# Conv weights built on GpSimd, only the borders of the conv input cleared, loads begun at once, last stores shared by two queues

## The chip, the cores and the metric

The kernel runs on 1 core of one Trainium2 chip. The metric is the time of one execution on the device, in microseconds (us). The engines are TensorE (PE in the profile), VectorE (DVE), ScalarE (ACT), GpSimd (POOL) and SyncE (SP); SP and ACT also issue DMAs, each on a queue of its own.

## The reference

One pre-activation layer, `x + attention(groupnorm(x))`, over x of shape (8, 512, 128, 128), f32. The 512 channels are 32 groups of 16, so there are 256 (image, group) pairs, all independent:

```
x = x + conv_ref(_gn(x), ...)
# conv_ref, for each group gx of 16 channels:
gap, gmp = mean(gx), max(gx) over (h, w)
channel_weight = sigmoid(gn(conv1x1([gap, gmp], w_cc, b_cc)))
hw = conv1x1([mean over w, mean over h], w_s1, b_s1)
pos_h, pos_w = sigmoid(conv1x1(hw[:h], w_ph, b_ph)), sigmoid(conv1x1(hw[h:], w_pw, b_pw))
sx = conv3x3(gx * pos_h * pos_w, w_s3, b_s3)      # 16 -> 16 channels, zero padding
spatial_weight = sigmoid(gn(sx))                  # per channel over (h, w)
out = gx * (channel_weight * spatial_weight)
```

## The kernel before, in words

**Layout.** A group (16 channels of 128x128) fills the 128 partitions: 16 channels times 8 row phases, with 16 rows of 128 pixels in each partition. A unit is two groups, j = 0 and 1, in 2 MB of `xt`; there are 128 units, and `xt` holds six of them. One group comes in by 8 DMAs of 128 KB, one for each row phase, and goes out by 8.

**Turns.** `turns` writes the program out for t = -5 to 128. In turn t the engines work on different units: t + 3 (unit e, row sums and maxima on DVE), t + 2 (c, position sums), t + 1 (a, gates, gate products on POOL, `modulate` on DVE), t (the 3x3 convolution on PE, its eviction on ACT) and t - 1 (b, spatial gate and final sums). DVE has its first unit in turn -3, PE its first convolution in turn 0; turn 128 (`t == UNITS`) only finishes unit 127. Every engine runs its list in order and waits on semaphores; nothing is scheduled at run time.

**Queues.** SP loads the weights (three DMAs), then group j = 1 of each unit, and stores everything. Its loads of units 0 to 5 wait for nothing, so 48 DMAs are issued in a row. ACT loads group j = 0 of each unit, spread over its compute; first it waits for the three weight DMAs (`w_in`) and seven memsets of POOL (`w_pool`), then issues units 0 and 1 (16 DMAs) and comes to `square1` of unit 0, which needs `negm` from DVE. Loads of unit 6 and later wait for `final` of the unit six earlier.

**Setup.** DVE expands every weight table from `weights` and `masks` with small instructions: `expand` makes a 128x128 table by four instructions of 128x32. The convolution's `W_conv` (three of 128x128) is nine expansions and six additions. The helper `link` makes DVE wait after each instruction for its own completion. PE then forms five products of tables (`w_pe`), DVE takes six results out of them, and clears the whole padded convolution input `gated` (9360 elements a partition), of which only the borders must be zero, since `gate_products` writes the inside of every unit. Only then does DVE turn to its first `row_sums`.

**End.** In turn 128 ACT runs, for unit 127: `variance2(b, 0)`, `square2(b, 1)`, `spatial_gate(b, 0)`, `variance2(b, 1)`, `spatial_gate(b, 1)`, `gate_plus_one(b, 1)`. `variance2` needs a product of PE and hands its value to POOL's `rstd2_power`, on which the `spatial_gate` of the same group waits. DVE follows with `gate_x` and `add_x` for j = 0, `gate_x` and `add_mean` for j = 1; each ends a group (`final`), and SP stores it.

## Time and profile before

| | |
|---|---|
| time, median of 3 runs | 3395.1 us (3390.4 to 3396.04) |
| time of the profiled execution | 3391.47 us |
| its span, first to last instruction | 3389.6 us |
| DVE busy | 97% of the span |
| PE busy | 95% |
| ACT busy | 90% |
| POOL busy | 75% |
| mean granted TensorE clock | 0.994 of full speed |

The span covers instructions alone; the time has 1.9 us more around it. Four numbers of this table (the three runs and the profiled one) lie within 5.7 us of each other for one and the same kernel.

### The profile page before, as it was taken

How to read it: one execution, taken by the hardware profiler on the slowest of the kernel's cores; microseconds unless marked ns; L12 is line 12 of the kernel's file. 1: busy time of each engine (PE TensorE's matmuls, PEld its weight loads, DVE VectorE, ACT ScalarE, POOL GpSimd, SP SyncE). 2: the span in 40 equal slices, each digit the busy share in tenths (PEclk: the TensorE clock that was granted, in tenths of full speed). 3: DMA queues.
4: the chain of work that ended last, by engine and by line, in shares of the span. 5: the costliest groups of instructions: out<-in, count | busy, mean ns of one | idle time of the engine just before them, and what ended most of it. 6: DMA issues, size and time to landing. Idle time of an engine off the chain costs nothing.

```text
span 3389.6 us, 125024 instructions
## 1 busy us (share of the span) xinstructions
PE 3212.1 (95%) x51732; PEld 1483.5 (44%) x51732; DVE 3288.2 (97%) x1997; ACT 3050.6 (90%) x5634; POOL 2542.6 (75%) x1548
## 2 busy tenths in 40 slices
PE   2999999999999999999999999999999999999996
PEld 1444444444444444444444444444444444444442
DVE  8999999999999999999999999999999999999984
ACT  1899999999999999999999999999999999999986
POOL 2777777887787777777787777777777777778872
PEclk9999999999999999999999999999999999999998
DMA  5467676776776767677677677667767767667755
GB/s 127 113 163 165 167 170 157 169 172 157 168 172 162 167 169 167 160 169 173 155 169 175 155 168 173 162 163 171 169 159 172 171 157 168 169 160 168 173 112 101
DMA packets 1115102, 545.32 MB, mean 161 GB/s; under 512 B 65712, under 2 KB 1114544, under 8 KB 1114544
## 3 DMA queue, kind: packets, MB, share of 16 engines
q1 hardware_dynamic: 836016, 403.05, 52.3%
q10 hardware_dynamic: 278528, 134.28, 14.9%
q8 instruction: 417, 6.83, 0.9%
q14 instruction: 141, 1.16, 0.1%
HBM read 268.63 MB, written 268.44 MB: 158 GB/s over the span
## 4 chain that ended last, share of the span: by engine, by line
DVE 58%; issue 23%; PE 7%; POOL 5%; ACT 3%; SPq 1%; DMA 1%; ACTq 1%; DVEq 0%; POOLq 0%
DVE mx L659 13%; DVE sp_buf L607 13%; DVE sums L644 12%; DVE gated L699 8%; DVE fold L632 6%; PE conv_ps L747 6%; DVE fold L636 2%; SPq L237 1%; DMA out<-sp_buf 1%; POOL rstd L327 1%; ACT sp_buf L393 1%; POOL rstd L266 1%; DVE sp_buf L617 1%; POOL var_e L308 1%; ACTq L382 1%
## 5 line engine op out<-in xcount | busy, mean ns | idle before, releaser
L747 PE MATMUL conv_ps<-gated,W_conv 64*32 64x512 f32 x49152 | 2803.4, 590 | 2.8 <-issue 1.6
L747 PEld LDWEIGHTS conv_ps<-gated,W_conv 64*32 64x32 f32 x49152 | 1126.3, 105 | 1492.5 <-issue 1461.2
L285 POOL TENSOR_TENSOR gated<-gate_w,gate_hr 128x2048 f32<-128x2048 f32 x256 | 1053.9, 4117 | 10.1
L393 ACT ACTIVATE sp_buf<-conv_ps,weights 128x512 f32<-128x512 f32 x1024 | 692.0, 678 | 148.3 <-DMA out<-sp_buf 120.6
L607 DVE SCALAR_TENSOR_TENSOR sp_buf<-xt,negm,sp_buf 128x2048 f32<-128x2048 f32 x256 | 600.3, 2345 | 42.6 <-ACT sp_buf L455 26.8
L699 DVE SCALAR_TENSOR_TENSOR gated<-xt,negm,gated 128x2048 f32<-128x2048 f32 x256 | 594.8, 2364 | 13.9 <-POOL gated L285 13.9
L327 POOL TENSOR_TENSOR rstd<-var_e,consts 128x4 f32<-128x4 f32 x129 | 389.0, 3015 | 273.4 <-DVE var_e L686 273.2
L644 DVE TENSOR_REDUCE sums<-xt 128x32 f32<-128x4096 f32 x128 | 564.9, 4413 | 0.1
L659 DVE TENSOR_REDUCE mx<-xt 128x2 f32<-128x4096 f32 x128 | 564.4, 4409 | 0.2 <-issue 0.2
L447 ACT ACTIVATE sp_buf<-sp_buf,bias,scale 128x2048 f32<-128x2048 f32 x256 | 536.9, 2097 | 8.5
L465 ACT ACTIVATE junk<-xt,negm 128x2048 bf16<-128x2048 f32 x256 | 512.5, 2002 | 28.3 <-DVE negm L693 28.3
L416 ACT ACTIVATE junk<-sp_buf,negm 128x2048 bf16<-128x2048 f32 x256 | 512.8, 2003 | 8.3
L266 POOL TENSOR_TENSOR rstd<-var_e,consts 128x1 f32<-128x1 f32 x256 | 305.4, 1193 | 246.5 <-ACT var_e L430 246.5
L617 DVE SCALAR_TENSOR_TENSOR sp_buf<-sp_buf,kfac,xt 128x2048 f32<-128x2048 f32 x128 | 301.1, 2352 | 4.5
L632 DVE TENSOR_TENSOR fold<-xt 128x2048 f32<-128x2048 f32 x128 | 292.1, 2282 | 0.0
L455 ACT ACTIVATE sp_buf<-sp_buf,consts,kfac 128x2048 f32<-128x2048 f32 x128 | 268.7, 2099 | 4.3
L308 POOL TENSOR_TENSOR var_e<-ch,consts 128x2 f32<-128x2 f32 x128 | 261.0, 2039 | 10.1 <-POOL ch L304 0.2
L274 POOL TENSOR_TENSOR gate_hr<-gate_h,rstd 128x32 f32<-128x32 f32 x128 | 114.1, 891 | 190.7 <-ACT gate_w L480 175.2
L393 ACT ACTIVATION_READ_ACCUMULATOR sp_buf<-conv_ps,weights 128x1 f32 x1024 | 201.4, 197 | 0.0
L295 POOL TENSOR_TENSOR fold<-fold 128x512 f32<-128x512 f32 x128 | 164.0, 1281 | 47.4 <-DVE fold L636 47.4
L747 PE MATMUL gn_ps<-late_in,M_chan 128*128 128x21 f32 x264 | 53.7, 281 | 129.4 <-ACT sp_buf L393 83.0
L626 DVE TENSOR_SCALAR sp_buf<-sp_buf,negm 128x2048 f32<-128x2048 f32 x128 | 164.7, 1287 | 4.5
(84 smaller groups left out, 2256.0 us busy)
## 6 DMA issues: line engine op xcount, KB each, us to landing
out<-sp_buf SPq DMA_DIRECT2D x2048, 128.0 KB, 2.8
xt<-in_x SPq DMA_DIRECT2D x1024, 128.0 KB, 3.7
xt<-in_x ACTq DMA_DIRECT2D x1024, 128.0 KB, 3.6
weights<-in_by_channel SPq DMA_DIRECT2D x1, 116.5 KB, 2.1
S_chan<-in_same_channel SPq DMA_DIRECT2D x1, 64.0 KB, 1.9
masks<-in_row_masks SPq DMA_DIRECT2D x1, 12.0 KB, 2.1
```

What stands on the lines that cost most here:

```text
L285: nc.gpsimd.tensor_tensor(gated[:, d, j, 1:1 + NB, 1:1 + W], gate_w[:, d, j].unsqueeze(1).to_broadcast([P, NB, W]), gate_hr[:, d, j].unsqu ...
L327: nc.gpsimd.tensor_tensor(rstd[:, s, first:4], var_e[:, s % 2, first:4], consts[:, first:4], ALU.pow).then_inc(rstd_done, 1)
L393: nc.scalar.activation(sp_buf[:, g, k * BB:(k + 1) * BB], conv_ps[:, k], ACT.Identity, bias=V["b_s3"], accum_out=sums2).then_inc(evac, 1)
L416: nc.scalar.activation(junk[:, 2], sp_buf[:, g].rearrange("p b w -> p (b w)"), ACT.Square, bias=negm2[:, g:g + 1], accum_out=squares).then ...
L447: nc.scalar.activation(flat, flat, ACT.Sigmoid, scale=scale2[:, g:g + 1], bias=bias2[:, g:g + 1]).then_inc(sig2, 1)
L465: nc.scalar.activation(junk[:, j], xt[:, s, j].rearrange("p b w -> p (b w)"), ACT.Square, bias=negm[:, s, j:j + 1], accum_out=all_in[:, (s ...
L607: nc.vector.scalar_tensor_tensor(flat, xt[:, s, j].rearrange("p b w -> p (b w)"), negm[:, s, j:j + 1], flat, ALU.add, ALU.mult).then_inc(f ...
L632: nc.vector.tensor_tensor(fold8[:], xt[:, s, :, 0:8], xt[:, s, :, 8:16], ALU.add).then_inc(fold8_done, 1)
L644: nc.vector.tensor_reduce(sums[:, s % 2].rearrange("p j b -> p (j b)"), xt[:, s].rearrange("p j b w -> p (j b) w"), AX_X, ALU.add).then_in ...
L659: nc.vector.tensor_reduce(mx[:, s % 2], xt[:, s].rearrange("p j b w -> p j (b w)"), AX_X, ALU.max).then_inc(mx_done, 1)
L699: nc.vector.scalar_tensor_tensor(inner, xt[:, s, j], negm[:, s, j:j + 1], inner, ALU.add, ALU.mult).then_inc(mod_done, 1)
L747: return nc.tensor.matmul(ps, lhsT, rhs, start=start, stop=stop)
```

## The change

Four things, all in the first turns or the last.

1. `W_conv` is expanded by POOL (36 small multiplications, then two additions over all 384 columns), after DVE has done its own tables. PE waits for it (`w_conv`) ahead of its first convolution.
2. POOL clears the borders of `gated` with four memsets; DVE's memset of all of it is gone. `link` no longer waits; DVE waits once inside its tables and once ahead of the six results, and these are taken in turn -3, behind the first `row_sums` and `totals`.
3. ACT's wait for `w_in` and `w_pool` moves from its beginning to turn -2, so its first 16 loads wait for nothing; a one-column Sigmoid (`warm`) follows that wait.
4. In turn 128 `variance2(b, 1)` comes ahead of `spatial_gate(b, 0)`, and the last unit's 16 stores are split: for each group SP issues four and ACT, after its last activation, four.

```diff
+            for s in range(2):
+                nc.gpsimd.memset(gated[:, s, :, 0:NB + 2:NB + 1, :], 0.0).then_inc(w_pool, 1)
+                nc.gpsimd.memset(gated[:, s, :, 1:1 + NB, 0:WP:WP - 1], 0.0).then_inc(w_pool, 1)
+            pool.wait_ge(w_pool, POOL_SETUP)
             pool.wait_ge(w_in, 16 * W_LOADS)
+            pool.wait_ge(w_dve, DVE_FIRST)
+            for kw in range(KW):
+                made = expand_conv(W_conv[:, kw], wconv_rep[:, kw, 1], masks[:, 1], made)
+                for i, kh in enumerate((0, 2)):
+                    made = expand_conv(w_part[:, i, kw], wconv_rep[:, kw, kh], masks[:, kh], made)
+            for i in range(2):
+                pool.wait_ge(w_conv, made)
+                nc.gpsimd.tensor_tensor(W_conv[:], W_conv[:], w_part[:, i], ALU.add).then_inc(w_conv, 1)
...
         def _(act):
-            act.wait_ge(w_in, 16 * W_LOADS)
-            act.wait_ge(w_pool, 7)
...
+                if t == -2:
+                    act.wait_ge(w_in, 16 * W_LOADS)
+                    act.wait_ge(w_pool, POOL_SETUP)
+                    nc.scalar.activation(warm[:, :], consts[:, 8:9], ACT.Sigmoid)
...
+                if t == UNITS:
+                    variance2(b, sb_, 1)
                 if real(b):
                     spatial_gate(b, sb_, 0)
...
-                if real(b):
+                if real(b) and t < UNITS:
                     variance2(b, sb_, 1)
...
             turns(act, body)
+            last_stores()
...
                 made[0] += 1
                 ins.then_inc(w_dve, 1)
-                dve.wait_ge(w_dve, made[0])
...
-            for kw in range(KW):
-                expand(W_conv[:, kw], wconv_rep[:, kw, 1], masks[:, 1])
-                for i, kh in enumerate((0, 2)):
-                    expand(w_part[:, i, kw], wconv_rep[:, kw, kh], masks[:, kh])
-                    link(nc.vector.tensor_tensor(W_conv[:, kw], W_conv[:, kw], w_part[:, i, kw], ALU.add))
...
-            link(nc.vector.memset(gated[:].rearrange("p s j b w -> p (s j b w)"), 0.0))
...
+                    if t == 0 and n == 0:
+                        pe.wait_ge(w_conv, CONV_SETUP)
```

DVE's program, from the last tables to the first `maxima`; before:

```order
L588 TENSOR_SCALAR mask_pix<-masks 128x8 [waits w_dve]
L590 COPY W_rows_m<-pos_ps 128x128 [waits w_pe,w_dve]
L591 COPY W_cols_m<-pos_ps 128x128 [waits w_dve]
L592 TENSOR_SCALAR W_rows<-pos_ps 128x128 [waits w_dve]
L593 TENSOR_SCALAR W_cols<-pos_ps 128x128 [waits w_dve]
L594 TENSOR_TENSOR W_gap_m<-W_gap_m,norm_ps 128x128 [waits w_dve]
L595 TENSOR_TENSOR b_pos<-pos_ps,weights 128x2 [waits w_dve]
L597 MEMSET gated 128x9360 [waits w_dve]
L644 TENSOR_REDUCE sums<-xt 128x32 [waits x_in01,x_in00,w_dve]
L653 TENSOR_REDUCE all_in<-sums 128x2 [waits sums_done]
L659 TENSOR_REDUCE mx<-xt 128x2
```

and of the change, the same place (its line numbers are 48 or 49 higher in the turns):

```order
L631 TENSOR_TENSOR W_ch_m<-W_gap,W_gmp 128x128 [waits w_dve]
L632 TENSOR_SCALAR W_gap_m<-W_gap 128x128
L693 TENSOR_REDUCE sums<-xt 128x32 [waits x_in01,x_in00,w_pool]
L702 TENSOR_REDUCE all_in<-sums 128x2 [waits sums_done]
L640 COPY W_rows_m<-pos_ps 128x128 [waits w_dve,w_pe]
L641 COPY W_cols_m<-pos_ps 128x128
L642 TENSOR_SCALAR W_rows<-pos_ps 128x128
L643 TENSOR_SCALAR W_cols<-pos_ps 128x128
L644 TENSOR_TENSOR W_gap_m<-W_gap_m,norm_ps 128x128
L645 TENSOR_TENSOR b_pos<-pos_ps,weights 128x2
L708 TENSOR_REDUCE mx<-xt 128x2
```

The memset is gone, the six results stand behind the first two reductions, and the first reduction waits for both groups of unit 0 (`x_in00`, `x_in01`).

ACT's program at the very end, unit 127; before:

```order
L416 ACTIVATE junk,late_in<-sp_buf,negm 128x2048 [waits sq2_done,evac,negm2_done]
L439 ACTIVATE scale<-rstd,weights 128x1 [waits sig2,rstd2_done]
L442 ACTIVATE bias<-negm,weights,scale 128x1 [waits aff2]
L447 ACTIVATE sp_buf<-sp_buf,bias,scale 128x2048 [waits sq2_done,aff2]
L430 ACTIVATE var_e<-gn_ps,consts 128x1 [waits rstd2_done,late_mm]
L439 ACTIVATE scale<-rstd,weights 128x1 [waits sig2,rstd2_done]
L442 ACTIVATE bias<-negm,weights,scale 128x1 [waits aff2]
L447 ACTIVATE sp_buf<-sp_buf,bias,scale 128x2048 [waits sq2_done,aff2]
L455 ACTIVATE sp_buf<-sp_buf,consts,kfac 128x2048 [waits kfac_done,sig2]
```

and of the change:

```order
L457 ACTIVATE junk,late_in<-sp_buf,negm 128x2048 [waits sq2_done,evac,negm2_done]
L471 ACTIVATE var_e<-gn_ps,consts 128x1 [waits rstd2_done,late_mm]
L480 ACTIVATE scale<-rstd,weights 128x1 [waits sig2,rstd2_done]
L483 ACTIVATE bias<-negm,weights,scale 128x1 [waits aff2]
L488 ACTIVATE sp_buf<-sp_buf,bias,scale 128x2048 [waits sq2_done,aff2]
L480 ACTIVATE scale<-rstd,weights 128x1 [waits sig2,rstd2_done]
L483 ACTIVATE bias<-negm,weights,scale 128x1 [waits aff2]
L488 ACTIVATE sp_buf<-sp_buf,bias,scale 128x2048 [waits sq2_done,aff2]
L496 ACTIVATE sp_buf<-sp_buf,consts,kfac 128x2048 [waits kfac_done,sig2]
L423 DMA out<-sp_buf 256x1x128 [waits final]
L423 DMA out<-sp_buf 256x1x128 x3
```

The variance of the last group (`var_e<-gn_ps`) has moved ahead of the other group's scale, bias and Sigmoid, and stores follow the last activation.

## Rows read from the trace of the kernel before

**Rows 1.** Windows, mid-run: busy PE, PEld, DVE, ACT, POOL; clock, DMA share, GB/s.

```profile
1000.00:1026.00 26.00, 25.27 (x420) 11.49 (x412) 25.82 (x16) 24.20 (x46) 19.75 (x13) 1.00 0.67 163
```

**Rows 2.** Timeline of DVE, setup: start us, busy us, line, operation, count, idle before.

```profile
3.81 0.87 DVE L565 TENSOR_TENSOR W_conv<-weights,masks 128x32 f32<-128x32 f32 x4 [3.81 <-DMA masks<-in_row_masks]
...
13.89 0.87 DVE L565 TENSOR_TENSOR W_s1h<-weights,masks 128x32 f32<-128x32 f32 x4
...
20.09 0.17 DVE L588 TENSOR_SCALAR mask_pix<-masks 128x8 f32<-128x8 f32 x1
22.73 0.29 DVE L590 COPY W_rows_m<-pos_ps 128x128 f32<-128x128 f32 x1 [2.46 <-PE pos_ps L740]
...
26.52 7.86 DVE L597 MEMSET gated<- 128x9360 f32 x1 [2.02 <-issue]
34.42 4.42 DVE L644 TENSOR_REDUCE sums<-xt 128x32 f32<-128x4096 f32 x1
```

**Rows 3.** SP's line of loads, its first eight: ns, issue times, us to landing.

```profile
L229 SPq DMA_DIRECT2D xt<-in_x x8: 592/608/736, 2.1 to 6.8; - x8
...
DMA to landing us min/median/max: 2.7/4.1/5.8
```

**Rows 4.** The same view of ACT's line of loads, its first eight.

```profile
L382 ACTq DMA_DIRECT2D xt<-in_x x8: 622/630/680, 3.8 to 8.5; - x8
...
DMA to landing us min/median/max: 3.6/5.4/6.8
```

**Rows 5.** Windows again: loads on two queues, and the last stores on one.

```profile
10.00:12.00 2.00, 0.00 (x0) 0.00 (x0) 1.73 (x9) 0.00 (x0) 0.00 (x0) 1.00 1.23 226
...
3386.00:3388.00 2.00, 0.00 (x0) 0.00 (x0) 0.00 (x0) 0.00 (x0) 0.00 (x0) 0.50 1.00 199
```

**Rows 6.** Timeline of the whole core, turn -2 to turn 0.

```profile
48.56 1.27 POOL L295 TENSOR_TENSOR fold<-fold 128x512 f32<-128x512 f32 x1 [47.36 <-DVE fold L636]
...
58.48 0.61 PE L747 MATMUL pos_ps<-sums,W_rows 128*128 128x32 f32 x2
...
62.05 1.28 ACT L475 ACT_TABLE_LOAD   x1 [13.01 <-POOL rstd L327]
...
64.74 0.24 POOL L274 TENSOR_TENSOR gate_hr<-gate_h,rstd 128x32 f32<-128x32 f32 x1 [2.78 <-ACT gate_w L480]
65.06 7.17 POOL L285 TENSOR_TENSOR gated<-gate_w,gate_hr 128x2048 f32<-128x2048 f32 x2
...
71.46 0.81 DVE L664 TENSOR_TENSOR late_in<-mx,mask_pix 128x16 f32<-128x16 f32 x1
...
77.23 8.86 PE L747 MATMUL conv_ps<-gated,W_conv 64*32 64x512 f32 x120
```

**Rows 7.** One POOL line over the whole run: ns min/median/max.

```profile
L274 POOL TENSOR_TENSOR gate_hr<-gate_h,rstd x128: 238/970/1257, 64.7 to 3314.5; 128x32 f32<-128x32 f32 x128
```

**Rows 8.** Timeline of DVE: one step in turn 1 and in turn 2.

```profile
112.39 5.70 DVE L699 SCALAR_TENSOR_TENSOR gated<-xt,negm,gated 128x2048 f32<-128x2048 f32 x2
...
143.34 4.61 DVE L699 SCALAR_TENSOR_TENSOR gated<-xt,negm,gated 128x2048 f32<-128x2048 f32 x2
```

**Rows 9.** Timelines of the end, engine after engine: ACT, PE, DVE.

```profile
3367.63 0.28 ACT L439 ACTIVATE scale<-rstd,weights 128x1 f32<-128x1 f32 x1
...
3373.29 0.29 ACT L439 ACTIVATE scale<-rstd,weights 128x1 f32<-128x1 f32 x1 [2.68 <-POOL rstd L266]
...
3367.78 0.62 PE L747 MATMUL gn_ps<-late_in,M_chan 128*128 128x21 f32 x2 [2.63 <-ACT junk L416]
...
3378.36 2.35 DVE L607 SCALAR_TENSOR_TENSOR sp_buf<-xt,negm,sp_buf 128x2048 f32<-128x2048 f32 x1 [3.12 <-ACT sp_buf L455]
3380.74 1.29 DVE L626 TENSOR_SCALAR sp_buf<-sp_buf,negm 128x2048 f32<-128x2048 f32 x1
```

**Rows 10.** SP's line of stores, the last four: ns, issue times, landing.

```profile
L237 SPq DMA_DIRECT2D out<-sp_buf x4: 616/620/622, 3384.6 to 3386.6; - x4
...
DMA to landing us min/median/max: 2.5/2.5/2.5
```

More of the change, by code:

```diff
@@ L30 @@
 LATE = BANKS + 1 + 2 * RB
+POOL_SETUP = 11
+CONV_SETUP = KW * 3 * PAIRS + 2
+DVE_FIRST = 6 * PAIRS + 4
+DVE_SETUP = DVE_FIRST + 6
 def conv_attention(nc, x, by_channel, same_channel, row_masks, out):
@@ L52, in conv_attention @@
         junk = sb("junk", [P, 3, NB * W], BF16)
+        warm = sb("warm", [P, 1])
         weights = sb("weights", [P, by_channel.shape[1]])
@@ L117, in conv_attention @@
         w_pool = sem("w_pool")
+        w_conv = sem("w_conv")
         x_in = [[sem(f"x_in{s}{j}") for j in range(2)] for s in range(XS)]
@@ L235, in store @@
                         sp.wait_ge(final, 2 * u + j + 1)
-                        for r in ROW_ORDER:
+                        for r in ROW_ORDER[:RB // 2] if u == UNITS - 1 else ROW_ORDER:
                             sp.dma_start(to[r], sp_buf[row_partitions(r), g]).then_inc(stored[g], 16)
@@ L255, in _, with expand_conv @@
             nc.gpsimd.memset(late_in[:], 0.0).then_inc(w_pool, 1)
-            pool.wait_ge(w_pool, 7)
+            for s in range(2):
+                nc.gpsimd.memset(gated[:, s, :, 0:NB + 2:NB + 1, :], 0.0).then_inc(w_pool, 1)
+                nc.gpsimd.memset(gated[:, s, :, 1:1 + NB, 0:WP:WP - 1], 0.0).then_inc(w_pool, 1)
+            pool.wait_ge(w_pool, POOL_SETUP)
             pool.wait_ge(w_in, 16 * W_LOADS)
+            def expand_conv(dst, rep, mask, made):
+                by_row = mask.rearrange("p (q t) -> p q t", t=2)
+                for pair in range(PAIRS):
+                    nc.gpsimd.tensor_tensor(
+                        dst[:, QUAD * pair:QUAD * (pair + 1)].rearrange("p (o t) -> p o t", t=2),
+                        rep.unsqueeze(2).to_broadcast([P, CG, 2]),
+                        by_row[:, pair].unsqueeze(1).to_broadcast([P, CG, 2]), ALU.mult).then_inc(w_conv, 1)
+                return made + PAIRS
+            pool.wait_ge(w_dve, DVE_FIRST)
+            made = 0
+            for kw in range(KW):
[5 more added lines that the diff above has]
+                nc.gpsimd.tensor_tensor(W_conv[:], W_conv[:], w_part[:, i], ALU.add).then_inc(w_conv, 1)
+                made += 1
+            assert made == CONV_SETUP
             def rstd2_power(u, s, j):
@@ L382, in load, with last_stores @@
                         act.dma_start(xt[row_partitions(r), vs, 0], come[r]).then_inc(x_in[vs][0], 16)
+            def last_stores():
+                u = UNITS - 1
+                s = u % XS
+                for j in range(2):
+                    g = 2 * (s % 2) + j
+                    at = (2 * u + j) * CG * PIX
+                    first = out_g[0, 0]
+                    act.wait_ge(final, 2 * u + j + 1)
+                    for r in ROW_ORDER[RB // 2:]:
+                        to = bass.AP(tensor=first.tensor, offset=at + r * W, ap=[list(d) for d in first.ap])
+                        act.dma_start(to, sp_buf[row_partitions(r), g]).then_inc(stored[g], 16)
             def evacuate(u, s, n):
@@ L584, in _, with products_taken @@
                         rep.unsqueeze(2).to_broadcast([P, CG, 2]), 1.0 / RB, None, ALU.mult))
+            link(nc.vector.tensor_scalar(M_chan[:, :], S_chan[:, :], 1.0 / PIX, None, ALU.mult))
+            link(nc.vector.tensor_scalar(mask_pix[:, :], masks[:, 1], float(PIX), None, ALU.mult))
+            dve.wait_ge(w_dve, made[0])
             link(nc.vector.tensor_tensor(W_ch_m[:, :], W_gap[:, :], W_gmp[:, :], ALU.add))
             link(nc.vector.tensor_scalar(W_gap_m[:, :], W_gap[:, :], 1.0 / (NB * W), None, ALU.mult))
[L587 to L597 removed]
+            assert made[0] == DVE_FIRST
+            dve.wait_ge(w_pool, POOL_SETUP)
+            def products_taken():
+                dve.wait_ge(w_pe, 1)
+                dve.wait_ge(w_dve, DVE_FIRST)
+                link(nc.vector.tensor_copy(W_rows_m[:, :], pos_ps[:, 0:P]))
+                link(nc.vector.tensor_copy(W_cols_m[:, :], pos_ps[:, P:2 * P]))
+                link(nc.vector.tensor_scalar(W_rows[:, :], pos_ps[:, 0:P], 1.0 / W, None, ALU.mult))
+                link(nc.vector.tensor_scalar(W_cols[:, :], pos_ps[:, P:2 * P], 1.0 / NB, None, ALU.mult))
+                link(nc.vector.tensor_tensor(W_gap_m[:, :], W_gap_m[:, :], norm_ps[:, 0:P], ALU.subtract))
+                link(nc.vector.tensor_tensor(b_pos[:, :], pos_ps[:, 2 * P:2 * P + 2], vec[:, 4:6], ALU.add))
+                assert made[0] == DVE_SETUP
             def gate_x(u, s, j):
@@ L709, in body @@
                     totals(e, se)
+                if t == -3:
+                    products_taken()
                 if real(c):
@@ L732, in _ @@
         def _(pe):
-            pe.wait_ge(w_dve, 70)
-            pe.wait_ge(w_pool, 7)
+            pe.wait_ge(w_dve, DVE_FIRST)
+            pe.wait_ge(w_pool, POOL_SETUP)
             nc.tensor.matmul(norm_ps[:, 0:P], M_all[:, :], W_ch_m[:, :], start=True, stop=True)
@@ L741, in _ @@
                              stop=True).then_inc(w_pe, 1)
-            pe.wait_ge(w_dve, 77)
+            pe.wait_ge(w_dve, DVE_SETUP)
             pos = pos_ps[:, 0:2 * (NB + W)].rearrange("p (j n) -> p j n", j=2)
```

9 lines of the change are left out of this document (removed).

## The prediction

> **What bounds the kernel now.** I read the windows of mid-run first, then the timeline of DVE at the start, then the timelines of the end. In mid-run DVE is busy 25.82 of 26 us, more than a turn takes; PE has 25.27 and ACT 24.20 [rows 1]. So DVE's list of work, run without a gap, sets the pace, and whatever delays its first real instruction delays everything by as much. Nothing in the steady turns is touched by the change: the same instructions stand there in the same order on every engine. What can move is the time until DVE begins unit 0, what the first turns wait for, and the drain behind the last unit.
>
> At the start the reader is to see DVE alone at work: tables from 3.81 us on, a wait of 2.46 us for PE's five products, six results, an idle 2.02 us that no engine ended, the 7.86 us memset, and only at 34.42 us the first reduction over x [rows 2]. Its input had long been there. SP's eighth load of unit 0 is issued at 6.8 and takes 5.8, so it lands at 12.6 us [rows 3]; ACT's eighth is issued at 8.5 and takes 6.8, so it lands at 15.3 us [rows 4]. The unit was complete 19 us before DVE looked at it.
>
> At the end the chain is: ACT's last gate, DVE's last two steps, SP's eight stores. The last final sum ends at 3380.74 + 1.29 = 3382.03 [rows 9], the last store is issued at 3386.6 and lands 2.5 us later, at 3389.1 [rows 10], against a span of 3389.6 and a time of 3391.5 us for this execution.
>
> **The change at the start, step by step.** *Removed from DVE ahead of `row_sums`:* the conv tables, 3.81 to 13.89 = 10.1 us (42 instructions); the memset with the idle time ahead of it, 7.86 + 2.02 = 9.9 us; the wait for PE, 2.5 us, since the products now run while DVE is waiting or reducing; and the six results, which move behind the first reductions [rows 2]. What is left are 28 small instructions that took 13.89 to 20.26 = 6.4 us with a wait in each [rows 2]. So DVE would be ready at 3.8 + 6.4 = 10.2 us at the latest. I needn't know how much quicker they run without the waits, because x is not there by then: from now on the loads of unit 0 set the start.
>
> *When unit 0 is complete.* SP's first x load is issued at 2.1 us behind three weight loads of some 0.4 us each [rows 3], so an engine's first DMA can go at about 0.8, and ACT's will, 3 us sooner than its 3.8 [rows 4]. It shares the DMA engines with SP, whose three weight loads and first x loads it will slow. The limit is bytes: 0.2 MB of weights (128 x 385 columns) and 2.1 MB of x, and with both queues full 226 GB/s [rows 5], which is 10.1 us after the first data at some 2.5 to 3.5 us, so 12.6 to 13.6, and a little of unit 1 goes ahead of it. From below, SP's group already landed at 12.6 with ACT starting later, so it won't be sooner; from above, the old 15.3. I take 14.0. DVE then starts 34.42 - 14.0 = **20.4 us** sooner, with 19.1 and 21.8 as bounds. The weights may land some us later than 3.8 for the same reason; there are 14.0 - 10.2 = 3.8 us of cover for that, and more if the waits shorten the tables.
>
> *Six results, now after the reduction:* they took 22.73 to 26.52 - 2.02 = 24.50, so 1.8 us with waits [rows 2]. Without them I take 1.6 (bounds 1.0 and 1.8). They are now between `totals` and `maxima`, on the path: **-1.6 us**.
>
> *The idle 2.02 us:* the trace gives no releaser for it. If it belongs to the memset it is gone; if DVE was waiting for its own instructions it may return elsewhere. DVE now has a wait for x of some us in which that would vanish, so I cost it at nothing, and at 2 us in the range.
>
> *POOL.* Four small memsets follow late_in's and are done within a few us. Then 36 expansions of 128x32 and two additions over 384 columns. The nearest row is POOL's other 128x32 multiplication: 0.24 us at least, 0.97 in the median [rows 7]; the additions lie near the 128x512 one at 1.27 [rows 6]. I take the low end, since the one of 0.24 at 64.74 [rows 6] lay beside a reduction of DVE (unit 2's row sums), and here too DVE waits or reduces: 36 x 0.24 + 2 x 1.27 = 11.2 us from at most 10.2, so done at 21.4. What waits for it: `fold_columns` of unit 0, which stood at 48.56 and would now stand near 30, and PE's first convolution, 77.23, now near 57.5 [rows 6]. Both covered, so cost nothing; PE only has one more wait in its list.
>
> The Trainium skill ("SBUF — State Buffer", its table of advice on running DVE and GpSimd together) says that where DVE has two SBUF inputs while the GpSimd operation reads SBUF, the second to issue blocks until the first ends. By that rule the reductions, with one input, block nothing, and the 0.24 us beside one agrees; under two-input work the expansions would be near the median instead. It bears on the second rival below.
>
> *The Sigmoid ahead of time.* Before, ACT's table load of 1.28 us at 62.05 stood between `rstd` and the gates of unit 0; POOL's gate products ended at 65.06 + 7.17 = 72.23, and DVE's `late_in`, from 71.46 to 72.27, ended only with them, though it computes 16 columns [rows 6]. With the table loaded in turn -2, under DVE's work, POOL is done 1.3 us sooner. DVE can use what it waited there, which I estimate at 0.6 of the 0.81, PE's position products that follow up to 1.3. I take **+0.7 us** (0 to 1.3).
>
> ACT's loads of unit 2 follow `square1` of unit 0, so come 19 us sooner, while SP still issues its 48 loads (0.61 us each at best [rows 3], so until 31 at least). Eight of them at half of 226 GB/s take 9.3 us: issued from about 26, there by 37, needed by the third reduction, two turns of 14.1 us behind the first (34.42 to 48.56, where unit 0's last step ended [rows 2, 6]), at 14.0 + 1.6 + 28 = 43.6. Covered too.
>
> Start: 20.4 - 1.6 + 0.7 = **19.5 us**.
>
> **The change at the end.** `variance2(b, 1)` needs PE's product, which ends at 3367.78 + 0.62 = 3368.4 [rows 9]. It now runs there, at about 3368.7 done, and only then does ACT start the scale of j = 0, at 3368.7 instead of 3367.63: +1.1 us for j = 0. POOL's power for j = 1 then runs while DVE is idle and under ACT's Sigmoid, not beside DVE's `gate_x`, so ACT's 2.68 us of waiting for it is gone [rows 9]. ACT reaches j = 1's scale 2.8 - 1.1 = 1.7 us sooner, and everything behind it too: ACT's last activation ends near 3376.6, DVE's j = 0 steps, which ended 3.12 before 3378.36 = 3375.24, now end at 3376.3, just before, and the last final sum comes at 3380.3.
>
> Stores: one queue needed 3389.1 - 3382.03 = 7.1 us. A group is 1.05 MB, which at 199 GB/s [rows 5] is 5.3 us: data flow from 1.8 us after the final sum. Split over two queues the issue takes four times 0.62 instead of eight, but then bytes bound: j = 0 is final at 3376.3, so 2.1 MB flow from 3378.1. At 199 GB/s they end at 3388.6, a gain of 0.5; at the 226 GB/s that two queues reached with loads they end at 3387.4, a gain of 1.7; were bytes no bound, 3380.3 + 3 x 0.62 + 2.5 = 3384.7, a gain of 4.4. I take **1.7 us**, as the loads' row shows two queues above one.
>
> The Trainium skill ("DMA: Bandwidth & Descriptors", Issuing engines are not separate DMA queues) speaks against this: starting DMAs from several engines saves only the sequencer's time, the 16 DMA engines being the same. By that rule the end gains 0.5 instead of 1.7, the sum 20.0 instead of 21.2. The loads' 226 against 199 speaks the other way, but those are reads.
>
> **Sum.** 19.5 + 1.7 = 21.2 us. Against the profiled execution, 3391.5 - 21.2 = 3370.3; against the median shown, 3395.1 - 21.2 = 3373.9. The four executions average 3393.3, and I forecast from there: **3372 us**.
>
> **Rivals.**
> 1. *POOL is late.* If each expansion takes the 0.97 us of the median row, POOL needs 36 x 0.97 + 2.5 = 37.5 us and is done at 47.7; `fold_columns` ends at 49, and PE's position products, at 58.48 before [rows 6], would stand at 39.7 and wait 9 us. The gain shrinks to 12: 3381 us. It decides from some 0.7 us an expansion on. For it: 0.97 is the median. Against it: in mid-run POOL mostly meets two-input DVE work, here none. 7%.
> 2. *The start gives nothing,* because the first turns already wait for something whose time the change leaves alone, such as loads that SP and ACT, both early, hand each other late. Then only the end is left: 3391 us. Against it: of the loads only those of unit 0 come within 5 us of being needed. 4%.
> 3. *Slower, by a lasting collision of POOL and DVE.* In turn 1 DVE's two `modulate` steps took 5.70 us, and from turn 2 on 4.61 [rows 8], 1.1 us more while POOL's products lay beside them. The change moves POOL against DVE by the table load's 1.3 us. Should the new phase keep the collision, each turn costs 1.1: 128 turns 140 us, 3512 us; it passes no-change after 20 turns and is measurably slower after 26. For it: DVE has no slack in which to absorb it [rows 1]. Against it: POOL moves away from the collision, not into it, and the old start, further in, had left it after two turns. 3%.
> 4. *More than forecast,* over 28 us: only if PE's first turns, which are not bound by DVE alone, shorten as well. 3%.
>
> **Numbers.** The forecast itself has 83%. Its bounds: start 16.3 (19.1 - 1.8 + 0, and 2 for the idle time returning, less 1 if weights delay the tables) to 22.1 (21.8 - 1.0 + 1.3), end 0.5 to 4.4, so 16 to 26.5, and three runs' median can lie 2 us either way of the mean. From 3393.3 this is 3365 to 3379, and the first rival begins above. A measurement tells about 0.2%, 6.8 us, from no change: faster is the forecast, rivals 1 and 4, less a little, 92%; same 5%; slower 3%.
>
> **What would show it.** DVE's first reduction near 14 us, released by a load of x and not by POOL or a memset; its tables ended by 10; POOL's additions done by some 22, with `fold_columns` waiting for DVE and not the reverse; no table load near turn -1; first convolution matmul near 57.5; the same 25.8 us a turn later on; the last final sum 1.7 us nearer the last activation chain, ACT's wait for `rstd` gone, DMA above 199 GB/s in the last 8 us. The prediction is wrong if unit 0 lands after 17, if POOL is still expanding at 40, or if the turns lengthen.

## The result, and the profile after

The changed kernel takes 3371.5 us (median of 6 runs, 3369.98 to 3374.94) against 3393.45 us for the kernel before (6 runs, 3390.4 to 3396.04): a ratio of 0.9937, with a 95% interval of 0.9927 to 0.9948, so 22 us faster. The profiled execution took 3370.14 us with a span of 3368.3, 21.3 less than before.

The start first: DVE's timeline of the changed kernel, which answers to [rows 2].

```profile
4.83 0.49 DVE L613 TENSOR_TENSOR W_s1h<-weights,masks 128x32 f32<-128x32 f32 x4 [4.83 <-DMA masks<-in_row_masks]
...
7.69 0.22 DVE L632 TENSOR_SCALAR W_gap_m<-W_gap 128x128 f32<-128x128 f32 x1
14.58 4.42 DVE L693 TENSOR_REDUCE sums<-xt 128x32 f32<-128x4096 f32 x1 [6.67 <-DMA xt<-in_x]
...
19.13 0.28 DVE L640 COPY W_rows_m<-pos_ps 128x128 f32<-128x128 f32 x1
...
20.19 4.41 DVE L708 TENSOR_REDUCE mx<-xt 128x2 f32<-128x4096 f32 x1
```

DVE is through its tables at 7.9 us and then idle for 6.67 us, until a load of x ends the wait. The first reduction is 19.8 us sooner, the first maximum, behind the six results, 18.8 (38.97 before, 20.19 now).

The other engines of the changed kernel in the same stretch, POOL, ACT and PE, beside [rows 6]:

```profile
8.08 0.83 POOL L272 TENSOR_TENSOR W_conv<-weights,masks 128x32 f32<-128x32 f32 x4 [5.73 <-DVE W_gap_m L632]
...
15.33 2.07 POOL L286 TENSOR_TENSOR W_conv<-W_conv,w_part 128x384 f32<-128x384 f32 x2
29.67 1.27 POOL L326 TENSOR_TENSOR fold<-fold 128x512 f32<-128x512 f32 x1 [12.27 <-DVE fold L685]
...
11.46 1.28 ACT L550 ACT_TABLE_LOAD   x1 [11.46 <-issue]
...
58.25 4.33 PE L797 MATMUL conv_ps<-gated,W_conv 64*32 64x512 f32 x44
```

POOL makes four expansions in 0.83 us, ends its additions at 17.4, and then waits 12.27 us for DVE. The table load lies in ACT's idle time. The first convolution matmul comes at 58.25 instead of 77.23, 19.0 sooner.

The end of the changed kernel, ACT, POOL and DVE, beside [rows 9]:

```profile
3348.85 0.26 ACT L471 ACTIVATE var_e<-gn_ps,consts 128x1 f32<-128x1 f32 x1 [0.71 <-PE gn_ps L797]
3349.01 0.28 ACT L480 ACTIVATE scale<-rstd,weights 128x1 f32<-128x1 f32 x1
...
3351.74 0.28 ACT L480 ACTIVATE scale<-rstd,weights 128x1 f32<-128x1 f32 x1
...
3349.19 0.55 POOL L297 TENSOR_TENSOR rstd<-var_e,consts 128x1 f32<-128x1 f32 x1 [1.81 <-ACT var_e L471]
...
3356.80 2.35 DVE L656 SCALAR_TENSOR_TENSOR sp_buf<-xt,negm,sp_buf 128x2048 f32<-128x2048 f32 x1 [0.19 <-ACT sp_buf L496]
3359.18 1.29 DVE L675 TENSOR_SCALAR sp_buf<-sp_buf,negm 128x2048 f32<-128x2048 f32 x1
```

ACT no longer waits for POOL between the two scales, and DVE's last wait for ACT has shrunk from 3.12 us to 0.19. The last final sum ends at 3360.47, and the span 7.8 us later, where it was 7.6 before (3382.03 and 3389.6).

In between the steady turns are as they were: from DVE's 128 maxima I read the length of each turn, and its median is 25.61 us in both kernels.

### The profile page after: what moved, and what is told of

Read it like the earlier page. It is cut to its first block, busy times and chain, and to the rows that moved or that the text cites. A ratio compares the mean times of both kernels' runs of the same rounds, so it can differ in the third digit from the quotient of the medians.

```text
span 3368.3 us, 125023 instructions
## 1 busy us (share of the span) xinstructions
PE 3213.9 (95%) x51732; PEld 1479.3 (44%) x51732; DVE 3266.7 (97%) x1954; ACT 3051.5 (91%) x5634; POOL 2553.3 (76%) x1590
## 4 chain that ended last, share of the span: by engine, by line
DVE 57%; issue 23%; POOL 6%; PE 6%; ACT 3%; SPq 2%; DMA 2%; ACTq 1%; DVEq 0%; POOLq 0%
DVE mx L708 13%; DVE sp_buf L656 13%; DVE sums L693 12%; DVE gated L748 8%; DVE fold L681 6%; PE conv_ps L797 5%; DVE fold L685 2%; SPq L243 2%; POOL rstd L358 1%; DMA out<-sp_buf 1%; POOL rstd L297 1%; POOL var_e L339 1%; DVE sp_buf L666 1%; ACT sp_buf L434 1%; POOL gated L316 1%
## 5 line engine op out<-in xcount | busy, mean ns | idle before, releaser
L506 ACT ACTIVATE junk<-xt,negm 128x2048 bf16<-128x2048 f32 x256 | 512.5, 2002 | 13.2 <-DVE negm L742 13.2
L339 POOL TENSOR_TENSOR var_e<-ch,consts 128x2 f32<-128x2 f32 x128 | 264.6, 2067 | 10.2 <-POOL ch L335 0.3
```

The lines of the kernel that those rows point to most:

```text
L506: nc.scalar.activation(junk[:, j], xt[:, s, j].rearrange("p b w -> p (b w)"), ACT.Square, bias=negm[:, s, j:j + 1], accum_out=all_in[:, (s ...
```

## The experiments

Each is compared by its marks in the trace: the start of DVE's first reduction, the first convolution matmul, the end of the last final sum, and the end of the span. Without any edit these are 14.58, 58.25, 3360.47 and 3368.3 us. The marks of the first 60 us repeat within some tenths of a microsecond, the time of a whole execution only within 5 us (the last section has most of it). Eight kernels, those without a ratio below, were timed once and are read by their marks alone; their times, in the order in which they follow, are 3371.5, 3371.8, 3373.4, 3376.6, 3386.8, 3388.5, 3378.8 and 3368.7 us.

**The start alone.**

```diff
-                if t == UNITS:
-                    variance2(b, sb_, 1)
...
-                if real(b) and t < UNITS:
+                if real(b):
...
-                        for r in ROW_ORDER[:RB // 2] if u == UNITS - 1 else ROW_ORDER:
+                        for r in ROW_ORDER:
...
-            last_stores()
```

> The change without its two edits at the end (the variance stays behind the other group's gate, SP issues all last stores). Theory: the start gives nearly all. First reduction of DVE again at about 14.6 us, first convolution matmul at about 58.3, last final sum 1.9 us later than in the whole change relative to the first convolution, so at about 3362.4, span 3370.0 (1.7 above the whole change, 19.6 below before), time ratio to before 0.994. Rival: the end gives more than it looked, since ACT's wait of 2.7 us is gone there and SP's stores halve; then the span is 3372 or more.

Measured: ratio to before 0.9937 (0.9921 to 0.9954), median 3372.38 against 3396.21 us; first reduction 14.34, first convolution matmul 58.01, span 3370.8. The last two steps of DVE in this kernel:

```profile
3359.60 2.35 DVE L653 SCALAR_TENSOR_TENSOR sp_buf<-xt,negm,sp_buf 128x2048 f32<-128x2048 f32 x1 [3.13 <-ACT sp_buf L496]
3361.98 1.28 DVE L672 TENSOR_SCALAR sp_buf<-sp_buf,negm 128x2048 f32<-128x2048 f32 x1
```

The wait of 3.13 us is back. From the start of ACT's last square (3346.87) to the end of the last final sum (3363.26) it is 16.4 us; in the change 14.4 (3346.05 to 3360.47). So the reordering gives 2.0 us and the start gives the rest, which is nearly everything. The span is 0.8 above the expected 3370.0; from the first convolution matmul to that square this execution took 3288.9 us, the change's 3287.8.

**The end alone**, on the kernel before: the same lines the other way round.

> The kernel before with the two edits at the end alone. Theory: first reduction at 34.4 us as before, last final sum 1.9 us sooner than before, at 3380.1, span near 3388, time ratio 0.9995, which the timing alone can't tell from 1. Rival: the two ends don't add (the last queue drain takes back what the reordering gives), span 3389.5.

Measured: ratio 0.9993 (0.9984 to 1.0002), so not to be told from 1 by time; first reduction 34.12, last final sum 3381.22, span 3389.2. The same two steps:

```profile
3377.54 2.35 DVE L623 SCALAR_TENSOR_TENSOR sp_buf<-xt,negm,sp_buf 128x2048 f32<-128x2048 f32 x1 [0.19 <-ACT sp_buf L468]
3379.93 1.29 DVE L642 TENSOR_SCALAR sp_buf<-sp_buf,negm 128x2048 f32<-128x2048 f32 x1
```

From the last square (3366.79) it is 14.4 us again, so the 2.0 us are there. The span is only 0.4 shorter, nearer to the rival's 3389.5 than to the theory's 3388. Most of that lies in between: from the first convolution matmul to the last square this execution took 3289.8 us, the kernel before 3288.4. A part is the rival's: the drain behind the last final sum took 8.0 us instead of 7.6.

**One queue for the last stores.** SP issues all 16; the reordering stays.

```diff
-                        for r in ROW_ORDER[:RB // 2] if u == UNITS - 1 else ROW_ORDER:
+                        for r in ROW_ORDER:
...
-            last_stores()
```

> The whole change, but SP issues all 16 of the last unit's stores. Theory (bytes bound, and two queues move more bytes a microsecond): last final sum at 3360.5 as in the change, GB/s near 200 in the drain instead of 230 to 245, and the span ends 8.5 to 9 us behind the last final sum instead of 7.8: about 1 us longer. Rival (the Trainium skill, DMA: Bandwidth & Descriptors, Issuing engines are not separate DMA queues: a second issuing engine saves only issue time): the same GB/s and 7.8 us.

Measured: last final sum 3360.76, span 3369.7, so 8.9 us behind it and not 7.8 (7.7 to 8.0 in all kernels with both edits). A window of the drain in this kernel (last columns: granted clock, DMA share, GB/s):

```profile
3364.00:3366.00 2.00, 0.00 (x0) 0.00 (x0) 0.00 (x0) 0.00 (x0) 0.00 (x0) 0.50 1.00 198
```

and of the change, in which the windows of 2 us between 3360 and 3366 have 230 to 245 GB/s:

```profile
3364.00:3366.00 2.00, 0.00 (x0) 0.00 (x0) 0.00 (x0) 0.00 (x0) 0.00 (x0) 0.50 0.98 238
```

The split is worth 1.1 us, as the first theory said. But 198 GB/s is not what one queue can carry. SP alone issues a store of 128 KB (131072 bytes) every 0.66 us, which makes 198 GB/s, and in the kernel before every store lands 2.5 us after its issue, the last like the first [rows 10]: nothing piles up. Where transfers had piled up, SP's queue alone moved more. These are windows of the kernel before, in its setup; ACT's first 16 loads have landed by 24.4 us, its next is issued at 44.96:

```profile
24.50:28.50 4.00, 0.00 (x0) 0.00 (x0) 1.98 (x2) 0.00 (x0) 0.00 (x0) 1.00 1.22 247
...
36.50:38.50 2.00, 0.00 (x0) 0.00 (x0) 2.00 (x1) 0.00 (x0) 0.00 (x0) 1.00 0.68 199
```

In the first, SP's loads land 4.1 to 5.0 us after their issue, in the second the last ones land 2.6 to 2.9 us after it: once the pile is gone, the pace of issuing (0.65 us a load) is the limit again. With two queues the last stores do pile up, as ACT's eight in the change show (ns of one issue, landing in us):

```profile
L423 ACTq DMA_DIRECT2D out<-sp_buf x8: 655/938/1270, 3356.6 to 3363.7; - x8
...
DMA to landing us min/median/max: 3.9/4.1/4.1
```

So one queue went at the pace of SP's issuing, and two go at what the DMA engines move. The Trainium skill ("DMA: Bandwidth & Descriptors", Issuing engines are not separate DMA queues) says that a second issuing engine saves only the sequencer's time for starting DMAs, and the traces agree: it was that time, 0.66 us a store, that one queue lacked here. The rival above, the same GB/s, doesn't follow from it. No run has stores piled up on one queue, so for stores this is read from the pace and the constant landing alone; the DMA share of 1.00 beside 198 GB/s doesn't speak against it, since SP's loads alone reached 1.22.

**Loads behind the weights.**

```diff
         def _(act):
+            act.wait_ge(w_in, 16 * W_LOADS)
+            act.wait_ge(w_pool, POOL_SETUP)
...
                 if t == -2:
-                    act.wait_ge(w_in, 16 * W_LOADS)
-                    act.wait_ge(w_pool, POOL_SETUP)
```

> The whole change, but ACT waits for the weights and POOL's memsets before its first load, as before. Theory (unit 0 is bound by bytes, and the head start of ACT's queue is taken from SP's group): ACT's group lands last, at 15.3 to 15.6 us, first reduction there, 0.8 to 1.0 us later than with loads at once. Rival: the head start counts in full, first reduction 3 us later, at 17.6. Second rival: the order is immaterial, 14.6.

```profile
15.97 4.42 DVE L694 TENSOR_REDUCE sums<-xt 128x32 f32<-128x4096 f32 x1 [8.92 <-DMA xt<-in_x]
```

So says its DVE timeline: first reduction at 15.97, 1.4 us later than in the change, first convolution matmul 59.65. More than the 0.8 to 1.0 of the theory, less than half of the 3 us of the rival. The head start of 3 us is worth about half of itself, because SP's group of unit 0 pays for it: its eighth load landed at 7.0 + 6.0 = 13.0 us here (issue and landing in the view of SP's line of loads), and at about 14.5 with ACT ahead.

**The conv tables back on DVE**, without a wait in each instruction (POOL's 38 instructions go):

```diff
+            for kw in range(KW):
+                for dst, kh in ((W_conv[:, kw], 1), (w_part[:, 0, kw], 0), (w_part[:, 1, kw], 2)):
...
+                        nc.vector.tensor_tensor(
...
+            for i in range(2):
+                dve.wait_ge(w_conv, KW * 3 * PAIRS + i)
+                nc.vector.tensor_tensor(W_conv[:], W_conv[:], w_part[:, i], ALU.add).then_inc(w_conv, 1)
```

> The whole change, but the conv tables are expanded by DVE again, behind its own tables and without a wait in each (36 small multiplications at the 0.10 us that the change shows for the others, two additions over 384 columns at some 0.5 us): 4.7 us more. Theory (DVE only waits for unit 0 there): its tables end at 7.9 + 4.7 = 12.6 us, before the load at 14.6, first reduction at 14.6, nothing lost; moving them to POOL was worth nothing once the waits were gone. Rival: the tables on POOL are what the gain is made of; DVE's first reduction comes 4.7 us or, at the old pace, 10 us later.

The DVE timeline of this kernel:

```profile
11.91 1.15 DVE L622 TENSOR_TENSOR W_conv<-W_conv,w_part 128x384 f32<-128x384 f32 x2
14.26 4.42 DVE L682 TENSOR_REDUCE sums<-xt 128x32 f32<-128x4096 f32 x1 [1.20 <-DMA xt<-in_x]
```

The tables end at 13.1, DVE still waits 1.20 us for x, and the first convolution matmul is at 57.95. With the memset and the waits gone, moving them to POOL was worth nothing. The 10.1 us that they took in [rows 2] were in large part waits: 42 instructions then, 38 in 4.9 us now.

**No early Sigmoid.**

```diff
-                    nc.scalar.activation(warm[:, :], consts[:, 8:9], ACT.Sigmoid)
```

> The whole change without the early Sigmoid (ACT's waits stay in turn -2). Theory: a table load for the gates of unit 0 returns, 1.28 us, between POOL's rstd (ends 43.2 us) and the gates; gate products end at 53.6 instead of 52.3, DVE's modulate and the first convolution matmul start 0.6 to 1.3 us later than 58.25. Rival: ACT has the time free, first convolution unchanged at 58.25.

In its ACT timeline the table load is back, ahead of the gates of unit 0:

```profile
44.06 1.28 ACT L516 ACT_TABLE_LOAD   x1 [11.59 <-POOL rstd L358]
```

(A second one stands at 27.10, ahead of the first square; it costs nothing that the marks show.) First reduction here at 15.37, 0.8 us later than in the change for a reason of its own (the load), so I compare from there: reduction to first convolution matmul 43.87 us, in the change 43.67. But from DVE's third maximum to its fourth, between which the gates of unit 0 stand, it took 18.98 us as before the change (19.00), and 18.08 in the change: 0.9 us. DVE's timelines behind that third maximum, of this kernel and then of the change, show where they lie:

```profile
53.47 0.80 DVE L712 TENSOR_TENSOR late_in<-mx,mask_pix 128x16 f32<-128x16 f32 x1
54.20 5.68 DVE L747 SCALAR_TENSOR_TENSOR gated<-xt,negm,gated 128x2048 f32<-128x2048 f32 x2
```

```profile
52.66 0.97 DVE L713 TENSOR_TENSOR late_in<-mx,mask_pix 128x16 f32<-128x16 f32 x1
53.55 4.61 DVE L748 SCALAR_TENSOR_TENSOR gated<-xt,negm,gated 128x2048 f32<-128x2048 f32 x2
```

`late_in` is longer with the early Sigmoid, not shorter; the two `modulate` steps behind it are 1.07 us shorter. Here POOL's last step of `fold_columns`, 1.26 us long, starts with them at 54.20; in the change it starts at 52.34, beside `late_in`, and is over when they begin. That it is this step which lengthens them is read from the timing; no run moved it alone. The convolution profits by less (0.2), since it follows PE's position products. So the edit is worth something between 0.2 and 0.9 us, and no more can be read from this trace, for the next turn lost some 4 us to something else (the pace of the first convolution, last section).

**Only the memset**, on the kernel before: POOL clears the borders.

```diff
+            for s in range(2):
+                nc.gpsimd.memset(gated[:, s, :, 0:NB + 2:NB + 1, :], 0.0).then_inc(w_pool, 1)
+                nc.gpsimd.memset(gated[:, s, :, 1:1 + NB, 0:WP:WP - 1], 0.0).then_inc(w_pool, 1)
...
-            link(nc.vector.memset(gated[:].rearrange("p s j b w -> p (s j b w)"), 0.0))
+            dve.wait_ge(w_pool, 11)
```

> The kernel before, with only the memset changed: POOL clears the borders, DVE's memset is gone. Theory: the idle 2.02 us ahead of the memset belongs to it (its own instruction or semaphore), so the first reduction comes at 24.5 to 24.6 us, 9.9 sooner than 34.42. Rival: DVE was waiting there for its instructions, so an idle time of about 2 us stands ahead of the first reduction, at 26.5, only 7.9 sooner.

The DVE timeline:

```profile
24.04 0.16 DVE L598 TENSOR_TENSOR b_pos<-pos_ps,weights 128x2 f32<-128x2 f32 x1
24.24 4.42 DVE L647 TENSOR_REDUCE sums<-xt 128x32 f32<-128x4096 f32 x1
```

The reduction follows without a gap, 10.2 us sooner than in [rows 2], and so does the first convolution matmul, at 67.05. The idle 2.02 us went with the memset. The span, 3384.7, is only 4.9 shorter than before: this is one of the executions with a slow first convolution (last section).

**POOL five times over.**

```diff
+            for _ in range(REPEAT):
+                if made:
+                    pool.wait_ge(w_conv, made)
...
+                    made = expand_conv(W_conv[:, kw], wconv_rep[:, kw, 1], masks[:, 1], made)
```

> The whole change, but POOL makes the conv tables five times over (180 multiplications at 0.20 us, about 36 us). Theory (rival 1 of the prediction as a price list): POOL is done at 8.1 + 36 + 2.1 + some waits = 46.5 to 47 us, fold_columns of unit 0 ends at 48, PE's position products, at 39.7 in the change, wait until then and everything behind them is 8 us late: first convolution matmul at 64 to 67, span 6 to 9 us above the change. Rival: there is enough slack between the position products and the first gates that less than 2 us is lost.

Timelines of POOL, PE and DVE in this kernel:

```profile
49.45 2.06 POOL L290 TENSOR_TENSOR W_conv<-W_conv,w_part 128x384 f32<-128x384 f32 x2
51.47 1.26 POOL L330 TENSOR_TENSOR fold<-fold 128x512 f32<-128x512 f32 x1
...
52.83 0.61 PE L801 MATMUL pos_ps<-sums,W_rows 128*128 128x32 f32 x2 [12.95 <-issue]
...
52.84 1.23 DVE L689 TENSOR_TENSOR fold<-fold 128x1024 f32<-128x1024 f32 x1 [10.49 <-POOL fold L330]
56.72 4.42 DVE L697 TENSOR_REDUCE sums<-xt 128x32 f32<-128x4096 f32 x1 [2.66 <-PE pos_ps L801]
```

The mechanism of the theory holds, its size was low: 13.1 us lost at PE's position products (39.69 in the change) and at the first convolution matmul (71.40), not 8. POOL was done at 51.5 instead of 47, since DVE's two-input steps held it up, from 26 us and again from 40 us on (four expansions took 2.80 us at 40.25, 0.83 elsewhere), and DVE stood still for POOL as well. In the change POOL has 12.27 us to spare ahead of `fold_columns`, which ends at 30.9, 8.8 us before it is needed: 21.0 in all. Here POOL is done 34.1 us later, 13.1 more than that. The span, 3386.7, is 18.4 above the change's and not 6 to 9: these 13.1, some 4 for the slow first convolution of this execution (last section), and scatter.

**All of the setup on DVE**, but without waits and with the results behind the reductions: the conv tables as above, POOL clears no borders, and

```diff
+            nc.vector.memset(gated[:].rearrange("p s j b w -> p (s j b w)"), 0.0).then_inc(w_conv, 1)
             dve.wait_ge(w_pool, POOL_SETUP)
```

> The change, but DVE does all of the setup that it did before: conv tables and the memset of the whole of gated (7.86 us), without a wait in each instruction and with the six results behind the first reductions. Theory: tables end at 13.1 us as with the conv tables alone, memset to 21.0, first reduction at 21.0 instead of 14.3: 13.4 of the 20 us come from the waits and the order, 6.6 from work taken off DVE. Rival: the work taken off is the gain (18 us of it), first reduction near 32.

Its DVE timeline:

```profile
11.68 1.15 DVE L620 TENSOR_TENSOR W_conv<-W_conv,w_part 128x384 f32<-128x384 f32 x2
14.73 7.86 DVE L621 MEMSET gated<- 128x9360 f32 x1 [1.90 <-DMA xt<-in_x]
22.50 4.36 DVE L681 TENSOR_REDUCE sums<-xt 128x32 f32<-128x4096 f32 x1
```

First reduction at 22.50, first convolution matmul 66.12. An idle time of 1.90 us stands ahead of the memset again, which the theory had left out (21.0). Of the 20 us, 11.9 come from the waits and the order (34.42 to 22.50) and the other 8 from taking work off DVE. How these are shared depends on what goes first, since unit 0 isn't there before 14.3 to 14.6. With the memset gone the conv tables are worth nothing, as shown above. With the memset still there they would be: without their 4.9 us DVE would start at an estimated 17.6 (22.50 less 4.9), which leaves the memset some 3 us.

**The row sums of unit 0 by group.**

```diff
+                if u == 0:
+                    dve.wait_ge(x_in[s][0], come)
+                    nc.vector.tensor_reduce(sums[:, 0, 0], xt[:, s, 0], AX_X, ALU.add)
+                    dve.wait_ge(x_in[s][1], come)
+                    nc.vector.tensor_reduce(sums[:, 0, 1], xt[:, s, 1], AX_X, ALU.add).then_inc(sums_done, 1)
+                    return
```

> The change, with only the row sums of unit 0 in two instructions, group 0 (ACT's loads, landed at about 11.6 us) and then group 1. Theory: DVE reduces group 0 from 11.6 to 13.9 and group 1 from 14.5 to 16.8, so the row sums end 2.2 us sooner and first convolution matmul comes 2.2 us sooner, at 55.9. Rival: no gain, since the next thing waits for something else; 58.

Measured: group 0 from 11.59, group 1 from 13.99, first convolution matmul 55.54, 2.7 us sooner than in the change.

**Unit 0 in halves**, loads and reductions, and the change itself beside it on the same chip:

```diff
+                        if v == 0:
+                            for jj, rows in ((0, group(x_g, 0)), (1, come)):
+                                for r in ROW_ORDER[:RB // 2]:
+                                    sp.dma_start(xt[row_partitions(r), 0, jj], rows[r]).then_inc(x_in[0][jj], 16)
+                            return
...
+                    nc.vector.tensor_reduce(sums[:, 0, 0], xt[:, s, 0], AX_X, ALU.add)
+                    nc.vector.tensor_reduce(mx[:, 0, 0:1], xt[:, s, 0].rearrange("p b w -> p (b w)"), AX_X, ALU.max)
+                    dve.wait_ge(x_in[s][1], come)
+                    nc.vector.tensor_reduce(sums[:, 0, 1], xt[:, s, 1], AX_X, ALU.add).then_inc(sums_done, 1)
...
```

> The whole change once more, beside the next kernel on the same chip, as its yardstick. Expected: first reduction at 14.3 to 14.6 us, first convolution matmul at 58.0 to 58.3, ratio to before 0.9937 as measured.

> The change, with unit 0 loaded group by group (SP and ACT each issue four DMAs of group 0, then four of group 1) and reduced group by group: row sums and maximum of group 0, then the row sums of group 1, totals, the six results, the maximum of group 1. Theory (from 8 to 14.6 us DVE waits for bytes alone): group 0 has landed by 8.5 to 9.5 us and group 1 by 13.5 to 14.5, DVE's first reduction starts at 9, the last maximum ends at 18.5 instead of 24.6, everything is 5 to 6 us sooner than in the change (first convolution matmul at 52.5 to 53.5), ratio to before 0.992. Rival: unit 1, which is needed 5 to 6 us sooner too, isn't there (its last load lands near 24), so DVE waits there and only 3 us or less are left. Second rival: two reductions in place of one and the shorter DMAs cost what the halves bring, less than 1 us gained.

The DVE timeline of the halves:

```profile
9.99 2.29 DVE L705 TENSOR_REDUCE sums<-xt 128x16 f32<-128x2048 f32 x1 [2.14 <-DMA xt<-in_x]
12.20 2.28 DVE L706 TENSOR_REDUCE mx<-xt 128x1 f32<-128x2048 f32 x1
14.46 2.29 DVE L708 TENSOR_REDUCE sums<-xt 128x16 f32<-128x2048 f32 x1
...
17.94 2.28 DVE L730 TENSOR_REDUCE mx<-xt 128x1 f32<-128x2048 f32 x1
...
25.13 4.41 DVE L714 TENSOR_REDUCE sums<-xt 128x32 f32<-128x4096 f32 x1
```

DVE starts at 9.99 and has no gap up to unit 1 but the 1.2 us for PE's product that is in all of these kernels, and unit 1 is there when wanted. First convolution matmul at 53.87, against 58.10 in the change beside it: 4.2 us sooner, less than the 5 to 6 expected: group 0 landed at 10.0 and not at 9, and the six results (1.1 us), which also stand ahead of the last maximum, were not in the expected 18.5, where it ended at 20.2. Splitting the reductions alone, above, had already given 2.7 of the 4.2. By time: 3369.74 us (3366.24 to 3370.5) against 3373.71 (3369.53 to 3375.67); the ratios to before, 0.993 (0.9918 to 0.9943) and 0.994 (0.9926 to 0.9954), overlap. It has the earliest first convolution of the study; by time the gain over the change isn't clear of the scatter.

## Why the prediction was right, step by step

- *What bounds.* That the steady turns stay is shown, 25.61 us a turn before and after (the prediction's 25.8 is DVE's busy time in a window of 26 us, not a turn). That DVE's list of work sets their pace rests on its busy share; no run changed that list.
- *When unit 0 is complete.* Forecast 14.0 us, measured 14.58 (14.3 to 14.6 in six traces of kernels that left the loads alone, 15.4 in a seventh). DVE ready at 10.2 "at the latest": 7.9, although the weights landed 1.0 us later, at 4.83. That the load sets the start is shown by its releaser, and by the tables put back on DVE at no cost.
- *Six results.* Forecast 1.6 us, measured 20.19 - 19.13 = 1.1. The two misses, 0.6 and 0.5, cancel by luck: first maximum 18.8 us sooner, as the sum 20.4 - 1.6 said.
- *The idle 2 us* was costed at nothing, with its return in the range. It belongs to the memset: gone without it, there again with it.
- *POOL* at nothing: shown, with 8.8 us of slack at `fold_columns`. It was done at 17.4, sooner than the 21.4 forecast, for it began at 8.1 and not at 10.2, the additions were 1.0 us each and the expansions 0.20. Rival 1 is real as a mechanism, and was never near. (Where the prediction speaks of two-input work and sends the reader to its second rival, the first is meant.)
- *The Sigmoid.* Forecast 0.7 us, by a shorter stay of DVE in `late_in` and earlier position products. The size is in range (0.9 in the turn of the gates, 0.2 at the convolution), the path is not: `late_in` grew from 0.81 to 0.97 us, and what shrank are the `modulate` steps, from 5.68 to 4.61. For this term the size came right by luck.
- *The start in sum.* Forecast 19.5; 19.0 at the first convolution matmul.
- *The end.* ACT's wait for POOL gone and 1.7 us forecast for the last final sum: 2.0 shown. In sum 1.7 us forecast; 16.4 - 14.4 = 2.0 from the order less 0.3 for the longer drain (7.83 against 7.57 us), 1.7. The stores: the forecast had two queues above one, by 226 GB/s taken from the loads, and 230 to 245 were measured against 198. Its reading of 199 GB/s as a limit of bytes was wrong: that is SP's issuing, 128 KB every 0.66 us. So the 0.5 that it worked out by the rule of the Trainium skill came from that misreading and not from the rule, with which the traces agree.
- *The sum*, 21.2 us: 21.3 in the spans of the two profiled executions, 22 in the medians. The 21.3 are 19.0 at the start, 1.7 at the end and 0.6 of scatter between the first convolution matmul and the last square. That they come so near is luck too: the second execution of the change has a span of 3373.7, 15.9 below the kernel before.
- *The range.* Its lower bound for the start, 16.3, isn't what its terms give: 19.1 - 1.8 - 2 is 15.3, and one more off is 14.3. Nothing came near it.
- *Rivals 2 and 3* didn't come: no load of x but unit 0's was waited for, and the collision of POOL and DVE got rarer. Three pairs of `modulate` steps took 5.7 us at the start before, one does now, and in the steady turns it is 4.6 in both.

What the prediction left unsaid: it took the four parts as they came. Two of them, the conv tables on POOL once the memset was gone and most of the loads' head start, bought little; the waits in `link`, the order and the memset bought nearly all.

## What to carry to other kernels

Where one engine is busy all through, look at when it begins its first real work, and follow what that waits for: once the waits and the memset are gone, the next bound is a load, and everything cut beyond it is worth nothing until the load comes sooner. Price such a cut by the marks of a trace and not by the time alone, which here scatters by 5 us. When the load is the bound, split the first tile, so that both queues bring its first part and the engine starts on that. And before a rate of transfers is taken for a limit of bytes, look at the time from issue to landing: where it stays constant, nothing piles up, and the engine that issues may be what sets the rate.

## What was not expected of the hardware

**The pace of the first convolution.** Its first 120 matmuls took 8.3 to 9.0 us in nine of the fourteen traces and 12.65 to 13.2 in the other five: without the early Sigmoid, with only the memset changed, with POOL's work five times over, and both kernels of the last comparison (the halves and the change itself). PE's timeline of the change, the first execution and then the second:

```profile
55.41 2.05 PE L797 MATMUL pos_ps<-fold,W_cols 128*128 128x256 f32 x4
...
58.25 8.59 PE L797 MATMUL conv_ps<-gated,W_conv 64*32 64x512 f32 x120
67.31 10.89 PE L797 MATMUL conv_ps<-gated,W_conv 64*32 64x512 f32 x192
...
79.05 1.11 PE L797 MATMUL pos_ps<-fold,W_cols 128*128 128x256 f32 x4
```

```profile
58.10 13.21 PE L797 MATMUL conv_ps<-gated,W_conv 64*32 64x512 f32 x120
...
71.78 10.89 PE L797 MATMUL conv_ps<-gated,W_conv 64*32 64x512 f32 x192
```

The same program, 4.6 us apart. At the pace of the 192 that follow, 120 would take 6.8 us. So PE is slow at first in both and speeds up some microseconds into the convolution, later in the five traces; its four products ahead of it take 2.05 us and, once it is fast, 1.11. The windows of the granted clock tell only half of this. Windows of the kernel without the early Sigmoid, and of the second execution of the change, PE alone (matmuls, granted clock, DMA):

```profile
59.00:63.00 4.00, 4.00 (x21) 0.50 0.00 0
63.00:67.00 4.00, 4.00 (x36) 0.50 0.11 31
```

```profile
58.00:62.00 4.00, 4.00 (x21) 1.00 0.00 0
62.00:66.00 4.00, 4.00 (x36) 1.00 0.25 72
```

The same 21 and 36 matmuls, once at a granted 0.50 (1.2 GHz, the lower of two levels) and once at 1.00 (2.4 GHz); in the nine quick traces the first two stretches of 4 us hold 37 to 53 and 80 to 88. In three of the five the windows print half clock, in two they don't, and they print 1.00 beside the slow products in the nine as well. The 1.00 says little there, for it is printed also where the trace has no entry of the clock at all. The first entry of full clock that lasts begins within 1.5 us of the first convolution matmul in the nine (58.84 us in the change) and 8.8 to 9.9 us after it in the five (68.00 in its second execution), and in the five PE's pace rises there, from 8 to 12 convolution matmuls a microsecond to 16 to 20. So a late rise to the higher level goes with the slow start in all fourteen; that PE ran at the lower level until then is shown in three and concluded in the rest. PE's work ahead of it, the same few small products in all of them, doesn't decide when it rises, and what does stays open. The cost is paid once: DVE's turn there lasts 24.1 to 25.4 us instead of 20.3 to 21.0, some 4 us. It fell on the change and on the halves in their profiled executions of the last comparison alike, and is most of the 5.4 us by which the change's span was longer there (3373.7) than in its first execution (3368.3).

**The scatter of the whole.** From the first convolution matmul to ACT's last square it is 3288.4 us before, 3287.8 in the change, and 3287.8 to 3293.7 over the fourteen traces. Turns are 25.60 us but for a few in each trace that take up to 26.7; which ones was not traced to a cause.

**The idle time ahead of the memset**, 2.02 us before and with the end alone, 1.90 with all of the setup on DVE, none where DVE has no such memset. The trace names no releaser in the first two cases and a load of x in the third, for an instruction that doesn't wait for x, so its cause is open too.
